# A fused adaLN, causal attention and sparse FFN block: the compare of chosen experts, the b1 row, and the orders of four engines

## The reference

```python
mod = (_silu(L0_c) @ L0_wmod).reshape(L0_c.shape[0], 6, 1, -1)
sa, ca, ga, sb, cb, gb = (mod[:, 0], mod[:, 1], mod[:, 2], mod[:, 3], mod[:, 4], mod[:, 5])
ga = (2 * (ga >= 0) - 1) * jnp.maximum(jnp.abs(ga), 0.25)
gb = (2 * (gb >= 0) - 1) * jnp.maximum(jnp.abs(gb), 0.25)
h = _layernorm(x, axis=-1) * (1 + ca) + sa
x = x + ga * _L0_attn_ref(h, ...)      # one head, causal, 2048 x 2048 scores
h = _layernorm(x, axis=-1) * (1 + cb) + sb
x = x + gb * _L0_ffn_ref(h, ...)

# _L0_ffn_ref: 16 experts of 32 hidden channels, the best 4 of each token
prob = jax.nn.softmax(xf @ w_router + b_router, axis=-1)
_, idx = jax.lax.top_k(prob, TOP_K)
mask = (idx[:, :, None] == jnp.arange(N_BLOCKS)[None, None, :]).any(axis=1)
h = jax.nn.relu(jnp.einsum('nd,ebd->neb', xf, w1b) + b1b[None])
y = jnp.einsum('neb,ebd,ne->nd', h, w2b, mask) + b2[None, :]
```

## Time and profile before

| | us |
|---|---|
| median of three runs | 120.59 (120.54 to 122.88) |
| the profiled execution, its whole time | 120.65 |
| its span, from the first to the last instruction | 118.9 |
| PE busy in the span | 109.7 (92%) |
| DVE busy | 90.6 (76%) |
| POOL busy | 88.3 (74%) |
| ACT busy | 74.5 (63%) |

### The profile page before, as it was taken

The page is one execution under the profiler, slowest core; times in us unless marked ns, Lnnn a source line. Parts: engine busy times, 40 slices in busy tenths (PEclk is TensorE's granted clock), DMA queues, the critical chain, the costliest instruction groups (busy, mean ns, idle before and its releaser), DMA issues.

```text
span 118.9 us, 1980 instructions
## 1 busy us (share of the span) xinstructions
PE 109.7 (92%) x579; PEld 87.0 (73%) x579; DVE 90.6 (76%) x319; ACT 74.5 (63%) x158; POOL 88.3 (74%) x114
## 2 busy tenths in 40 slices
PE   5789999999998999979987999699998999999980
PEld 2467889788886888668775877588786878857770
DVE  5989999999999979759996969413599856856431
ACT  2244495799940898596567979788333578545430
POOL 6856799828999699999939689989995888932000
PEclk9999999999999999999999999999999999999999
DMA  2993000000000000000000000000000000011322
GB/s 50 269 348 88 3 0 6 0 0 0 0 6 0 6 0 0 0 3 0 0 0 0 6 0 0 0 0 0 0 0 0 6 6 0 0 37 52 88 88 88
DMA packets 5862, 3.41 MB, mean 29 GB/s; under 512 B 727, under 2 KB 5467, under 8 KB 5852
## 3 DMA queue, kind: packets, MB, share of 16 engines
q1 hardware_dynamic: 5420, 3.09, 8.7%
q10 hardware_dynamic: 432, 0.20, 0.7%
HBM read 2.24 MB, written 1.05 MB: 28 GB/s over the span
## 4 chain that ended last, share of the span: by engine, by line
PE 55%; POOL 19%; DVE 15%; issue 5%; ACT 3%; POOLq 0%; DVEq 0%; ACTq 0%
PE bank L883 10%; PE bank L887 9%; PE bank L884 9%; POOL p_lo L490 8%; PE bank L943 5%; PE bank L995 4%; PE bank L917 3%; POOL hid_lo L496 3%; PE bank L982 3%; DVE g_lo L734 3%; PE bank L983 3%; PE bank L1027 2%; DVE chosen L797 2%; DVE swung_sums L770 2%; PE bank L1115 2%
## 5 line engine op out<-in xcount | busy, mean ns | idle before, releaser
L490 POOL TENSOR_TENSOR p_lo<-p_full,p_hi 128x512 fp32r<-128x512 f32 (+2 forms) x36 | 43.6, 1234 | 7.7 <-ACT p_full L595 7.5
L588 ACT ACTIVATE p_hi<-bank 128x512 fp32r<-128x512 f32 (+2 forms) x36 | 20.7, 574 | 3.7 <-DVE bank L745 1.7
L595 ACT ACTIVATE p_full<-bank 128x512 f32<-128x512 f32 (+2 forms) x36 | 20.7, 575 | 2.3 <-POOL p_lo L490 2.2
L496 POOL TENSOR_TENSOR hid_lo<-hid_full,hid_hi 128x512 fp32r<-128x512 f32 x12 | 15.3, 1288 | 4.6 <-ACT hid_hi L622 4.6
L716 DVE TENSOR_REDUCE cmax<-bank 128x1 f32<-128x512 f32 x24 | 15.8, 683 | 1.8 <-PE bank L943 1.6
L995 PE MATMUL bank<-g_lo,zt_hi 128*128 128x512 f32 (+3 forms) x40 | 14.7, 374 | 1.0 <-DVE g_lo L734 1.0
L982 PE MATMUL bank<-g_hi,zt_hi 128*128 128x512 f32 (+3 forms) x40 | 15.1, 379 | 0.0
L983 PE MATMUL bank<-g_hi,zt_lo 128*128 128x512 f32 (+3 forms) x40 | 14.6, 364 | 0.0
L883 PE MATMUL bank<-p_hi,z_hi 128*128 128x512 f32 (+2 forms) x36 | 13.9, 386 | 0.0
L884 PE MATMUL bank<-p_hi,z_lo 128*128 128x512 f32 (+2 forms) x36 | 13.5, 374 | 0.0
L887 PE MATMUL bank<-p_lo,z_hi 128*128 128x512 f32 (+2 forms) x36 | 13.4, 373 | 0.0
(11 more groups left out here) (201 smaller groups left out, 258.0 us busy)
## 6 DMA issues: line engine op xcount, KB each, us to landing
x<-in_L_attn_y_all_dram SPq DMA_DIRECT2D x3, 256.0 KB, 3.2
out_dram<-res SPq DMA_DIRECT2D x3, 256.0 KB, 2.3
w<-in_L_ffn_w_dram SPq DMA_DIRECT2D x2, 256.0 KB, 4.0
x<-in_L_attn_y_all_dram SPq DMA_DIRECT2D x2, 128.0 KB, 2.9
wmod<-in_L_wmod_dram SPq DMA_DIRECT2D x1, 256.0 KB, 3.6
out_dram<-res SPq DMA_DIRECT2D x2, 128.0 KB, 1.8
wmod<-in_L_wmod_dram ACTq DMA_DIRECT2D x1, 128.0 KB, 2.6
wq<-in_L_attn_Wq_dram ACTq DMA_DIRECT2D x1, 64.0 KB, 2.9
```

The source lines that it names most:

```text
L490: pool.tensor_tensor(p_lo[:, s, w:], p_full[:, n % 2, w:], p_hi[:, s, w:].bitcast(F32), ALU.subtract).then_inc(p_lo_pool, 1)
L496: pool.tensor_tensor(hid_lo[:, m, :], hid_full[:, n % 2, :], hid_hi[:, m, :].bitcast(F32), ALU.subtract).then_inc(hid_lo_pool, 1)
L588: nc.scalar.activation(p_hi[:, s, w:], src, ACT.Exp).then_inc(p_hi_s, 1)
L595: nc.scalar.activation(p_full[:, n % 2, w:], src, ACT.Exp).then_inc(p_full_s, 1)
```

## The change

Three things change. First, `chosen` is no longer a compare of marked keys with a constant. For groups 0 to 2 DVE writes a second copy of each token's highest logit into PSUM (a reduction of 64 elements to 4), and the mask comes from a two-operand compare of the marked keys in SBUF with that maximum in PSUM. Second, z6 of DVE takes the product's row 0 from its bank in PSUM, adds b1 and writes row 0 of w1_full, instead of adding in place in SBUF; PE's first weighting w0, which overwrites that bank, waits for it. Third, all four order tables are written anew; of TENSOR_PLAN the diff shows three lines, of two others the lines in which a step moves that is spoken of below. In SCALAR_PLAN z9 moves ahead of n1 and z7 from behind e16 to behind e3.

```diff
 TENSOR_PLAN = """
...
-a21 w6 a22 w7 a23 w8 a24 w9 b2 w10 s12 a25 a26 s13 s14 a27 w11 s15 a28 a29 s16 s17 o1 w12 s18 s19 a30 a31 w13
-s20 a32 s21 w14 a33 a34 n4 w15 s22 a35 a36 s23 w16 a37 w17 w18 a38 a39 w19 w20 w21 b3 r0 s24 w22 s25 w23 s26 s27
-s28 m0 o2 n5 s29 w24 s30 w25 h0 r1 s31 s32 h1 s33 w26 w27 m1 w28 s34 n6 s35 w29 s36 w30 s37 s38 w31 s39 h2 w32
...
+a21 s11 a22 w7 a23 w8 a24 w9 b2 w10 w11 a25 s12 a26 s13 a27 s14 a28 a29 s15 w12 o1 s16 w13 a30 w14 a31 s17 s18
+s19 a32 w15 a33 w16 a34 s20 a35 n4 s21 a36 s22 a37 s23 w17 a38 a39 w18 w19 w20 b3 w21 r0 s24 w22 s25 h0 w23 s26
+s27 s28 m0 w24 s29 o2 n5 s30 w25 s31 r1 w26 w27 s32 w28 s33 h1 w29 m1 s34 w30 s35 n6 s36 s37 w31 h2 s38 r2 w32
...
 VECTOR_PLAN = """
-j0 z0 j1 z1 a0 a1 g1 z3 u0 u1 z10 g2 v1 s0 s1 s2 s3 q0 n1 b0 g3 q1 s4 s5 z5 s6 s7 s8 s9 s10 s11 n2 b1 x0 q2 s12
+j0 z0 j1 a0 z1 a1 g1 u0 z3 z10 u1 g2 v1 s0 s1 s2 s3 q0 n1 b0 z6 g3 s4 s5 z5 s6 s7 q1 s8 s9 s10 s11 n2 b1 x0 s12
...
 GPSIMD_PLAN = """
-z7 z0 z4 z8 j0 j1 z1 p1 p2 z6 u0 l0 l1 l2 p3 u1 l4 l5 l6 l7 l8 z11 l9 l10 z10 u2 l12 l13 l14 l15 l16 p4 l17 l18
+z7 z0 j0 j1 p1 z8 z1 p2 z6 u0 l0 l1 l2 p3 u1 u2 l4 l5 l6 l7 z11 l8 l9 l10 z10 z9 l12 l13 l14 p4 l15 l16 l17 l18
+l19 l20 l21 p5 l22 u3 l24 l25 l26 l27 l28 l29 p6 l30 l31 l32 l33 l34 k0 k1 l35 l36 l37 l38 k2 k3 k4 k5 p7 k6 k7
+k8 k9 k10 z4 k11
...
+        def highest(g):
+            return sums_bank(g)[:, GW // 2 + GT * NBLK:GW // 2 + GT * NBLK + GT]
...
                 step(nc.vector.tensor_reduce(logit, sums.rearrange("p i s e -> p i e s"), AX.X, ALU.add))
+                if g not in shut_by_tensor:
+                    nc.vector.tensor_reduce(highest(g), logit, AX.X, ALU.max)
                 step(nc.vector.tensor_reduce(lmax[:], logit, AX.X, ALU.max))
...
-                nc.vector.tensor_scalar(chosen[:], each, FURTHEST, None, ALU.is_ge).then_inc(chosen_s, 1)
+                nc.vector.tensor_tensor(chosen[:], each, highest(g).rearrange("p (i e o) -> p i e o", e=1, o=1).broadcast_to(
+                    [P, GT, NBLK, PER]), ALU.is_gt).then_inc(chosen_s, 1)
...
-                    bias = w1_full[0:1, :].rearrange("p (m q) -> p m q", m=NH)
-                    nc.vector.tensor_tensor(bias, bias, dealt(b1_row[:]), ALU.add).then_inc(w1_bias_s, 1)
+                    row0, up = (t.rearrange("p (m q) -> p m q", m=NH) for t in (w1_full[0:1, :], up_bank[0:1, :]))
+                    nc.vector.tensor_tensor(row0, up, dealt(b1_row[:]), ALU.add).then_inc(w1_bias_s, 1)
...
                 if t == 0:
-                    pe.wait_ge(w1_full_s, 1)
+                    pe.wait_ge(w1_bias_s, 1)
```

More of the change, by code:

```diff
@@ L43 @@
 TENSOR_PLAN = """
-i0 i2 i1 z0 z10 z1 n0 z2 z3 q0 z6 z4 p0 a0 a1 a2 a3 p2 n1 z7 b0 q1 p1 s0 s1 s2 a4 z5 a5 s3 a6 a7 w0 n2 a8 a9 w1
-w2 w3 a10 a11 p4 z9 p6 z8 b1 q2 o0 s4 n3 p5 a12 s5 a13 s6 s7 a14 w4 a15 a16 s8 s9 a17 w5 a18 s10 a19 q3 a20 s11
-a21 w6 a22 w7 a23 w8 a24 w9 b2 w10 s12 a25 a26 s13 s14 a27 w11 s15 a28 a29 s16 s17 o1 w12 s18 s19 a30 a31 w13
-s20 a32 s21 w14 a33 a34 n4 w15 s22 a35 a36 s23 w16 a37 w17 w18 a38 a39 w19 w20 w21 b3 r0 s24 w22 s25 w23 s26 s27
-s28 m0 o2 n5 s29 w24 s30 w25 h0 r1 s31 s32 h1 s33 w26 w27 m1 w28 s34 n6 s35 w29 s36 w30 s37 s38 w31 s39 h2 w32
@@ L49 @@
-w33 r2 h3 w34 w35 w36 w37 d0 w38 w39 h4 h5 d1 o3 m2 d2 d3 h6 h7 d4 d5 h8 h9 d6 n7 d7 h10 r3 y0 d8 h11 h12 m3 y1
-h13 v12 v13 d9 d10 d11 h14 v14 h15 v15 d12 d13 y2 d14 d15 d16 d17 d18 d19 y3 y4
+i1 i0 i2 z0 z10 z1 n0 z2 z3 z6 q0 z4 z7 a0 a1 a2 a3 n1 p2 p1 p0 b0 q1 s0 s1 s2 a4 a5 z5 s3 a6 a7 w0 n2 a8 w1 a9
+w2 w3 a10 p4 a11 z9 p6 z8 b1 q2 o0 s4 p5 a12 n3 s5 s6 a13 s7 a14 w4 a15 a16 s8 s9 a17 w5 a18 s10 a19 w6 a20 q3
+a21 s11 a22 w7 a23 w8 a24 w9 b2 w10 w11 a25 s12 a26 s13 a27 s14 a28 a29 s15 w12 o1 s16 w13 a30 w14 a31 s17 s18
@@ L51 @@
+s19 a32 w15 a33 w16 a34 s20 a35 n4 s21 a36 s22 a37 s23 w17 a38 a39 w18 w19 w20 b3 w21 r0 s24 w22 s25 h0 w23 s26
+s27 s28 m0 w24 s29 o2 n5 s30 w25 s31 r1 w26 w27 s32 w28 s33 h1 w29 m1 s34 w30 s35 n6 s36 s37 w31 h2 s38 r2 w32
+s39 h3 w33 w34 w35 w36 w37 w38 h4 m2 w39 h5 d0 o3 d1 d2 d3 h6 h7 d4 h8 h9 d5 d6 n7 h10 d7 r3 h11 d8 d9 h12 m3
+d10 y0 v12 h13 v13 y1 d11 h14 v14 h15 v15 d12 d13 y2 d14 d15 d16 d17 d18 d19 y3 y4
 """
 SCALAR_PLAN = """
-z0 z1 j0 j1 z3 q0 z6 z4 z11 n1 a2 q1 e0 z9 z5 e1 e2 e3 c0 n2 z12 a3 z8 q2 e4 e5 n3 e6 e7 e8 e9 e10 q3 e11 e12
@@ L54 @@
-e13 e14 c1 e15 e16 z7 e17 e18 a4 e19 e20 e21 n4 e22 e23 a5 e24 e25 c2 e26 m0 e27 e28 n5 e29 e30 h0 a6 e31 e32 m1
-e33 n6 e34 e35 e36 h1 e37 h2 e38 h3 e39 c3 h4 h5 m2 y0 h6 h7 a7 h8 n7 h9 h10 y1 m3 h11 h12 h13 y2 h14 h15 y3 y4
+z0 z1 j0 j1 z3 z11 z6 q0 z4 z9 n1 a2 q1 e0 e1 z5 e2 n2 e3 z7 c0 z12 a3 z8 q2 e4 e5 n3 e6 e7 e8 e9 e10 q3 e11 e12
+c1 e13 e14 e15 e16 a4 e17 e18 e19 e20 e21 n4 e22 a5 e23 e24 e25 c2 e26 m0 e27 e28 n5 e29 h0 e30 e31 a6 e32 e33
+m1 e34 h1 n6 e35 e36 e37 e38 e39 h2 h3 c3 h4 h5 m2 y0 h6 h7 a7 h8 n7 h9 h10 y1 m3 h11 h12 h13 y2 h14 h15 y3 y4
@@ L56 @@
 """
 VECTOR_PLAN = """
-j0 z0 j1 z1 a0 a1 g1 z3 u0 u1 z10 g2 v1 s0 s1 s2 s3 q0 n1 b0 g3 q1 s4 s5 z5 s6 s7 s8 s9 s10 s11 n2 b1 x0 q2 s12
-s13 s14 n3 s15 s16 i8 s17 i9 s18 s19 s20 i10 s21 s22 s23 s24 b2 i11 g4 s25 s26 s27 s28 s29 z6 x1 g5 s30 s31 s32
-i20 s33 i21 s34 s35 i22 i23 s36 s37 n4 s38 s39 q3 b3 m0 c0 x2 g6 n5 h0 m1 c1 h1 i36 i37 n6 h2 i38 i39 h3 m2 c2
+j0 z0 j1 a0 z1 a1 g1 u0 z3 z10 u1 g2 v1 s0 s1 s2 s3 q0 n1 b0 z6 g3 s4 s5 z5 s6 s7 q1 s8 s9 s10 s11 n2 b1 x0 s12
+q2 s13 s14 n3 s15 s16 i8 i9 s17 s18 s19 i10 s20 s21 i11 s22 s23 s24 b2 s25 s26 s27 s28 s29 g4 x1 q3 s30 g5 s31
@@ L61 @@
+s32 s33 s34 i20 s35 i21 s36 s37 i22 s38 s39 n4 i23 b3 m0 c0 h0 x2 n5 g6 m1 c1 h1 i36 n6 h2 i37 m2 i38 h3 i39 c2
 h4 h5 x3 g7 h6 h7 h8 h9 n7 h10 m3 c3 h11 f0 k12 k13 f1 k14 k15 f2 f3 f4
@@ L63 @@
 GPSIMD_PLAN = """
-z7 z0 z4 z8 j0 j1 z1 p1 p2 z6 u0 l0 l1 l2 p3 u1 l4 l5 l6 l7 l8 z11 l9 l10 z10 u2 l12 l13 l14 l15 l16 p4 l17 l18
-l19 l20 l21 p5 l22 z9 l24 l25 l26 l27 l28 p6 l29 l30 k0 l31 l32 l33 l34 l35 k1 u3 l36 l37 l38 k2 k3 k4 k5 p7 k6
-k7 k8 k9 k10 k11
+z7 z0 j0 j1 p1 z8 z1 p2 z6 u0 l0 l1 l2 p3 u1 u2 l4 l5 l6 l7 z11 l8 l9 l10 z10 z9 l12 l13 l14 p4 l15 l16 l17 l18
+l19 l20 l21 p5 l22 u3 l24 l25 l26 l27 l28 l29 p6 l30 l31 l32 l33 l34 k0 k1 l35 l36 l37 l38 k2 k3 k4 k5 p7 k6 k7
+k8 k9 k10 z4 k11
 """
```

## The result

The changed kernel takes 117.06 us as a median of four executions (116.43 to 118.43), beside 120.62 for the kernel before (120.54 to 122.88, four executions): the ratio is 0.969, 95% interval 0.961 to 0.977, so 2.3 to 3.9% faster. (Medians and ranges are of all executions; ratios compare the means of those within 1.5% of their kernel's fastest.) The prediction was 117.2 in a range of 115.9 to 119.7. The profiled execution is the longest of the four, 118.43 us with a span of 116.0; the others have spans of 114.7 or 114.8. Outside the span lie 2.43, 1.85, 1.73 and 2.76 us, where the kernel before has 1.67 to 2.07 in the executions beside the experiments.

The account below looks back on a forecast made before the run. Bound: PE's work plus its stops while POOL or DVE owns the chain. Stops of 4.09 us filled or gone, less 0.25 for z6 and 0.4 for POOL, gain 3.4: 117.2 us against 120.65, range 115.9 to 119.7.

Parts of the forecast that it names:

- six stops of the earlier trace: PE standing before score 12's and 24's third passes, norm 4's turning, m0, m1, o3: 4.54 us, 4.09 forecast filled or gone.
- The 0.4 that POOL was to take back: POOL, late next from 40.35 to 90.75 us: some idle time would stand again, 0.4 us off the gain, a judgement.
- I take 0.68: DVE's compare `chosen`, one operand in PSUM: 0.68 us instead of 1.28 to 1.59, from rows of like operands.
- m0 and m1: PE's stops of 0.88 and 1.06 us: gone through masks 0.38 and 0.57 earlier plus 0.69 of work before each.
- the cover: PE's h0 put before m0 and w29 before m1, to fill 0.69 us of each stop.
- o3: the hidden rows waited for POOL: PE's 0.50 us stop before o3, laid to POOL's 1.92 us u3; gone with u3 moved behind l22.
- Norm 4: PE's 0.78 us stop before norm 4's turning: gone, since p4 on POOL starts 2.9 us earlier, behind three subtractions.
- Cost: 0.25 us: z6's new place on DVE between step b of groups 0 and 1: 0.6 us less 0.35 idle, at most 0.6 lost.
- Score 12: PE's stop before score 12's third pass: w11 and a25 fill 0.35 of 0.70 us.
- Score 24: PE's stop before score 24's third pass: w21 behind b3 fills 0.52 of 0.62 us.
- 1.43 each: POOL's five subtractions around z6's old place, 7.17 us in all, read as 1.43 each against 1.32 later.
- I take 0: Start of the kernel: z4 leaving POOL's chain against DVE's a0 before z1, no net effect, 0.3 us either side.

Follow-up runs that it names:

- after: The changed kernel with the whole change, against the kernel before: 117.06 us beside 120.62, ratio 0.969; its profiled execution has a stretch of 71.38 us on PE.

## Why the prediction was right, and where it wasn't

The total holds: 3.4 us forecast, 3.56 by the medians. In part that is luck. The terms describe the span; it was forecast at 115.5 and is 114.7 or 114.8 in three of four executions, so 4.1 to 4.2 were won. The median comes back to the forecast because up to 2.76 us and not 1.75 lie outside the span, and because one execution began slowly.

By place the 4.1 us won in the stretch can be read from the two profiles. Of the six stops of the earlier trace rows, 4.54 us, 0.25 is left: 4.29 are gone where 4.09 were forecast. From score 0's third pass to b2 the stretch is 0.51 longer (21.77 instead of 21.26), where 0.25 was put down. The 0.4 that POOL was to take back didn't come. What is left, some 0.35 in favour of the new order, no bracket names.

- **"I take 0.68"** for the compare: right, 0.69. That the 1.3 to 1.6 us of the old one were blocking is right too. The Trainium skill's tier table ("VectorE: DVE Perf Modes", "The perf-mode tier table"), by which the new form is the slower one in itself, roughly fits what is left once POOL is done: 0.28 us for the old form, 0.55 for the two-operand form in SBUF. By my estimate from the table's figures for 2048 elements they would take 0.31 and 0.57. The new form wins all the same, since it is never held up: 0.686 to 0.690 in every profile. The Trainium skill's other rule ("SBUF — State Buffer", "Who interferes with whom"), that DVE and GpSimd exclude each other over a shared pair, is what the runs show: masks of 3.08 and 3.35 us, or 3.00 for POOL's pair. That the order of issue decides who waits, as it says, the starts here neither show nor refute.
- **m0 and m1, "Gone":** they are. But the compare and the cover were added up as if each were needed. Without the compare three of four spans stay at 114.7 to 114.9; without the cover 0.89 comes back. The compare's worth in the new orders is that the mask cannot get stuck behind POOL.
- **"o3: the hidden rows waited for POOL":** wrong. The compare alone, with u3 in its old place, removes that stop. The bracket names hid_full; the mask ahead of it on DVE was the late one, itself held up by POOL's pair, and u3's 1.92 us were not what held it. u3's move is worth 1.67, at the weightings.
- **Norm 4, "the stop is 0.78. It goes":** it does, but moved back alone the place costs 2.40. The step looked at the turning, and not at what is queued behind ACT's application. In the new order ACT reaches that application at 47.07 instead of 48.15 and waits for POOL's power until 50.60, and PE stops at a score that needs the exponentials behind it. It is the largest single term by this measure, sized at a third.
- **z6, "Cost: 0.25 us":** both halves off. The length is 1.06 and not 0.6, since `dealt` was overlooked, and the b1 cast comes 0.47 later relative to step b0 instead of some 0.3 (9.24 behind it instead of 8.77). Its old place, "worth nothing by themselves", stops PE for 1.09 in the new order through x1. The move gains 1.03 net where 0.25 was put down as a loss.
- **Score 12:** 0.25 left, somewhat less than said (0.35). **Score 24:** no bracket.
- **"1.43 each"** for POOL's five subtractions around the old z6: a misreading of a merged row. One took 2.16 us, beside z6, and the others 1.3. The two in the earlier trace rows that follow the masks, at 1.42 and 1.46, are of the same kind. Without such neighbours POOL needs 43.14 us in its stretch and not the 44.25 of the sum.
- **"For this I take 0.4 off":** not needed; POOL's idle time fell from 4.86 to 2.51 us, and PE waits for it nowhere in after.
- **The start, "I take 0":** right without the slow pace (15.67 against 15.78), 1.0 more with it, of which nothing was foreseen.

The moves undone one at a time give 1.03 + 0.89 + 2.40 + 1.67 = 5.99 us, more than the 4.1 won: each is undone among new neighbours, so that one undone move can cost what in the old order others hid. How the 4.1 divides among the moves can't be told. Not tried: the start of the new order with a0 behind z1.

## What to carry over

When a wait is removed, read what stands behind it on the waiting engine, not only who is named in the bracket: the name is that of the last writer, and the late one can be its neighbour in the queue. If an instruction of DVE varies in length while its work doesn't, look at when POOL's instruction beside it ends: here the time from that end to its own was always the same, 0.28 us, so the rest was waiting inside it. One operand in PSUM made its length fixed; that is worth most in the executions that would have gone wrong. Compare kernels over a stretch that leaves out the start and the last store, and bridge a pause in PE's first products with fillers before reading tenths.
